# Windowed attention layers: per-head 64x32 array tiles, scores and attention output in shared PSUM banks, and a new order of the tensor engine's work

## The reference

```
# per layer: 16 heads of width 64, windows of 32 tokens
qkv = shift_tokens(x) @ Wqkv                 # 128 -> 3 x 1024
q, k = l2norm(q) * qs, l2norm(k) * ksc, then rotary
# each window of 32 queries sees 64 keys: its own window and the one before
sim  = einsum('bhwie,bhwje->bhwij', bq, bk2) * 8
attn = softmax(where(mask, -big, sim))
out  = einsum('bhwij,bhwje->bhwie', attn, bv2) @ Wo
x = out + x
x = (a * gelu(gate)) @ W2 + b2 + x           # a, gate = norm(shift_tokens(x)) @ W1 + b1
```

## Time and profile before

| | |
|---|---|
| timed runs, median | 4777.45 us |
| profiled execution, its own time | 4780.14 us |
| its span, first to last instruction | 4778.4 us |
| mean granted PE clock | 0.962 |
| layers phase, first to last mask product | 615.5 to 4096.0 us |
| one turn in the steady state | 35.67 us |

### The profile page before, as it was taken

One profiled execution on the slowest core, in us unless ns is written; L12 is line 12 of the kernel. 1 busy time (PEld: TensorE's weight loads), 2 busy tenths in 40 slices (PEclk: granted clock), 3 DMA queues, 4 the chain that ended last, 5 costly groups with the idle time before them and its releaser, 6 DMA issues. The chain is left out here.

```text
span 4778.4 us, 118285 instructions
## 1 busy us (share of the span) xinstructions
PE 4447.2 (93%) x45408; PEld 3473.8 (73%) x45408; DVE 3626.2 (76%) x6437; ACT 3028.2 (63%) x4718; POOL 1788.6 (37%) x966
## 2 busy tenths in 40 slices
PE   7999589999999999999999999999999999689999
PEld 2333268887788877888778887788778888468778
DVE  6887588888788887878878888788888888466554
ACT  5777357676767766676667676776767676333333
POOL 0000155554555544555455554455445555000000
PEclk9988799999999999999999999999999999889999
DMA  0000122222322222222222222222222222100000
GB/s 28 5 5 5 47 59 60 56 54 51 84 53 57 60 57 70 59 60 52 69 64 58 54 59 70 59 58 59 56 69 61 59 57 55 62 7 5 9 7 5
DMA packets 132797, 229.65 MB, mean 48 GB/s; under 512 B 29080, under 2 KB 33824, under 8 KB 131104
## 3 DMA queue, kind: packets, MB, share of 16 engines
q1 hardware_dynamic: 132256, 222.28, 17.8%
HBM read 29.23 MB, written 4.19 MB: 7 GB/s over the span
## 5 line engine op out<-in xcount | busy, mean ns | idle before, releaser
L660 POOL TENSOR_TENSOR qk_rotated<-qk_rotated,rotary_sines 128x1024 f32<-128x1024 f32 x384 | 923.5, 2405 | 1693.1 <-DVE rotary_sines L748 1693.1
L671 POOL TENSOR_TENSOR qk_rotated<-qk_rotated,rnorm 128x1024 f32<-128x1024 f32 x384 | 733.7, 1911 | 7.4
L756 DVE TENSOR_REDUCE qk_sumsq<-qk_squared 128x16 f32<-128x1024 f32 x384 | 467.4, 1217 | 296.5 <-ACT qk_squared L502 296.5
L221 PE MATMUL ps_proj<-qkv_w_hi,x_shifted_hi 128*128 128x512 f32 x1152 | 493.8, 429 | 38.7 <-DVE qkv_w_lo L716 24.0
L509 ACT ACTIVATE q_t<-ps_qk_t 128x512 f32<-128x512 f32 x384 | 229.7, 598 | 465.3 <-PE ps_qk_t L277 465.3
L738 DVE TENSOR_TENSOR qk_rotated<-ps_proj,rotary_scaled 128x1024 f32<-128x1024 f32 x384 | 467.4, 1217 | 7.6 <-ACT qk_squared L502 4.3
L748 DVE TENSOR_TENSOR rotary_sines<-ps_proj,rotary_scaled 128x1024 f32<-128x1024 f32 x384 | 466.0, 1213 | 1.7 <-POOL qk_rotated L660 1.7
L523 ACT ACTIVATE k_t_by_head<-ps_qk_t 64x512 f32<-64x512 f32 x768 | 452.1, 589 | 11.8 <-PE ps_qk_t L286 2.5
L223 PE MATMUL ps_proj<-qkv_w_hi,x_shifted_lo 128*128 128x512 f32 x1152 | 458.9, 398 | 0.0
L222 PE MATMUL ps_proj<-qkv_w_lo,x_shifted_hi 128*128 128x512 f32 x1152 | 457.4, 397 | 0.0
L502 ACT ACTIVATE qk_squared<-ps_proj 128x1024 f32<-128x1024 f32 x384 | 392.4, 1022 | 67.5 <-DVE qk_sumsq L756 49.8
(11 more groups left out here) (248 smaller groups left out, 9727.2 us busy)
## 6 DMA issues: line engine op xcount, KB each, us to landing
v_by_window<-v_tokens SPq DMA_DIRECT2D x1152, 128.0 KB, 2.4
v_by_window<-v_tokens SPq DMA_DIRECT2D x384, 64.0 KB, 2.1
v_by_window<-v_by_window SPq DMA_DIRECT2D x192, 64.0 KB, 2.0
qkv_w_raw<-in_layer_qk_dram SPq DMA_DIRECT2D x7, 1664.0 KB, 7.7
layer_w<-in_layer_w_dram SPq DMA_DIRECT2D x6, 580.5 KB, 3.8
layer_w<-in_layer_w_dram SPq DMA_DIRECT2D x6, 512.0 KB, 3.5
f_x<-in_x_dram SPq DMA_DIRECT2D x8, 256.0 KB, 6.2
x_attn<-f_y SPq DMA_DIRECT2D x8, 256.0 KB, 2.0
```

The costliest lines, as they stand in the source:

```text
L221: mm(out, hi, HI[:, o:o + 512], start=True, stop=False)
L660: tt(u, u, TB[:], ALU.add).then_inc(added, 1)
L671: tt(u, u, r.unsqueeze(3).broadcast_to((P, 2, 8, DH)), ALU.mult).then_inc(scaled, 1)
L756: nc.vector.reduce_sum(SS[:, 16 * i:16 * i + 16], SQ[:].rearrange("p (h e) -> p h e", e=DH), AX).then_inc(sumsq, 1)
```

## The change

Products: `score` and `pv` now treat each head by itself. The weights are 64 rows by 32 columns, the moving operand has 64 columns, and there are 32 products per group in place of 16 (64 records with their weight loads in place of 32). The two heads of a pair use the two halves of the rows. Scores and attention output of head z of each pair share one bank: `SA` is two banks, the first 256 columns of each are `S[z]`, the last 256 are `A[z]`. The mask product and `shift` become two products of 256 columns each. Keys and values lose the zero halves, and `k_t_out` is one copy of 128 partitions. All four transposes go through `TP`.

Order: `strips` waits for everything that scores and `pv` need ahead of the mask product. `out_t` moves ahead of `shift`; each of the projections `k0`, `v1`, `q1`, `k1` and `q0` is cut in two halves that stand around another piece, and `hidden01` is cut in `hidden0` and `hidden1` around `probs_t`. DVE does `norm_out` before `row_max`, and `row_max` also waits for `pv`. ACT does `out_t_out` before `exps`, and `high_part` moves up in slot 1.

```diff
-        TP, S, A, X = ps("ps_qk_t"), ps("ps_scores"), ps("ps_attention"), ps("ps_tail")
+        SA, TP, X = ps("ps_scores_attn", 2 * 512), ps("ps_transposed"), ps("ps_tail")
+        S = [SA[:, 512 * z:512 * z + 256] for z in range(2)]
+        A = [SA[:, 512 * z + 256:512 * z + 512] for z in range(2)]
...
+                for z in range(2):
+                    mm(S[z].rearrange("p (c k) -> p c k", k=DH), IDR[:], MASKR[:, g.t:g.t + 1, 0:DH].broadcast_to([P, 4, DH]), start=True, stop=False,
+                       skip_group_check=True)
                 for c in range(4):
-                    for w in range(4):
-                        q, k = g.t * P + WIN * w, base + WIN * w
-                        last = mm(S[WIN * w:WIN * w + WIN, c * P:(c + 1) * P], QT[:, 4 * g.half + c, q:q + WIN],
-                                  KD[:, :, 4 * g.half + c, k:k + 2 * WIN], start=False, stop=True, skip_group_check=True)
+                    for z in range(2):
+                        rows = slice(DH * z, DH * z + DH)
+                        for w in range(4):
+                            q, k = g.t * P + WIN * w, base + WIN * w
+                            last = mm(S[z][WIN * w:WIN * w + WIN, c * DH:(c + 1) * DH], QT[rows, 4 * g.half + c, q:q + WIN],
+                                      KT[rows, 4 * g.half + c, k:k + 2 * WIN], start=False, stop=True, skip_group_check=True)
...
+            def strips(scored, attended):
+                score_waits(scored)          # exps of the group before, q and k copied, halo
+                pv_waits(attended)           # probs copied, norm_out of the group before, values
+                score(scored)
+                pv(attended, scored.live)
...
+            def out_t(g, turned, scored):
+                if g.live:
+                    pe.wait_ge(o_norm, g.n + 1)
+                    if turned.live:
+                        pe.wait_ge(qt_out, turned.n + 1)
...
-                score(gs[0])
-                pv(ga[0])
-                q_t(gt[0])
-                shift(gs[0])
-                k0(n1)
-                out_t(ga[0])
-                k_t(gt[0])
-                v1(now, n1)
-                probs_t(gs[0])
+                strips(gs[0], ga[0])
+                q_t(gt[0], gs[0])
+                k0_first(n1)
+                out_t(ga[0], gt[0], gs[0])
+                shift(gs[0])
+                k0_second(n1)
+                k_t(gt[0], ga[0])            # now also waits for out_t_out
+                v1_first(now, n1)
+                probs_t(gs[0], gt[0], ga[0]) # now also waits for k_t_out
+                v1_second(now)
                 rstd_rows(h, e)
...
+                q_t(gt[1], gs[1])            # slot 1
+                q1_first(n1)
+                mean(e)
+                out_t(ga[1], gt[1], gs[1])
+                shift(gs[1])
+                q1_second(n1)
+                k_t(gt[1], ga[1])
+                hidden0(h, n1)
+                probs_t(gs[1], gt[1], ga[1])
+                hidden1(h)
...
+                hidden2(h, e)                # slot 2
+                out_t(ga[2], gt[2], gs[2])
+                shift(gs[2])
+                k1_first(n1, h)
+                k_t(gt[2], ga[2])
+                k1_second(n1)
...
+                wo_first(w)                  # slot 3
+                out_t(ga[3], gt[3], gs[3])
+                shift(gs[3])
+                q0_first(n2)
+                k_t(gt[3], ga[3])
+                q0_second(n2)
...
-                for h in range(2):           # ACT, k_t_out
-                    r = slice(DH * h, DH * h + DH)
-                    a(KD[r, h, 4 * g.half:4 * g.half + 4, base:base + P], TP[r, :].rearrange("p (c k) -> p c k", k=P),
-                      ACT.Copy).then_inc(kt_out, 1)
+                a(KT[:, 4 * g.half:4 * g.half + 4, base:base + P], TP[:].rearrange("p (c k) -> p c k", k=P), ACT.Copy).then_inc(kt_out, 1)
...
-                row_max(gs[0])               # DVE, slot 0; the other slots likewise
                 norm_out(ga[0])
+                row_max(gs[0], ga[0])
```

More of the change, by code:

```diff
@@ L214, in _, with project @@
             mm = nc.tensor.matmul
-            def project(m, t, x, bank, done):
-                for half in range(2):
+            def project(m, t, x, bank, done, halves=(0, 1)):
+                for half in halves:
                     out, o = bank[:, 512 * half:512 * half + 512], x * INNER + 512 * half
@@ L223, in project, with q0_first @@
                     last = mm(out, lo, HI[:, o:o + 512], start=False, stop=True)
-                last.then_inc(done, 1)
-            def q0(m):
+                    if half == 1:
+                        last.then_inc(done, 1)
+            def q0_first(m):
                 if m.live:
@@ L311, in shift @@
                     pe.wait_ge(nmax, g.n + 1)
[L312 to L315 removed]
+                    for z in range(2):
+                        last = mm(S[z].rearrange("p (c k) -> p c k", k=DH), IDR[:], NMX[:, 4 * z:4 * z + 4].unsqueeze(2).broadcast_to((P, 4, DH)),
+                                  start=False, stop=True, skip_group_check=True)
@@ L317, in probs_t @@
+                    last.then_inc(shifted, 1)
+            def probs_t(g, turned, attended):
                 if g.live:
                     pe.wait_ge(exped, g.n + 1)
+                    if turned.live:
+                        pe.wait_ge(kt_out, turned.n + 1)
+                    elif attended.live:
+                        pe.wait_ge(ot_out, attended.n + 1)
+                    after(pe, pt_out, g.n)
+                    for c in range(4):
+                        last = nc.tensor.transpose(TP[:, c * P:(c + 1) * P], E[:, g.k % 2, c * P:(c + 1) * P], IDENT[:])
+                    last.then_inc(pt_mm, 1)
@@ new lines, in pv @@
+            def pv(g, cleared):
+                if not g.live:
+                    return
+                for c in range(4):
+                    for z in range(2):
+                        rows = slice(DH * z, DH * z + DH)
+                        for w in range(4):
+                            o = c * P + WIN * w
+                            last = mm(A[z][WIN * w:WIN * w + WIN, c * DH:(c + 1) * DH], PT[rows, o:o + WIN],
+                                      V2[rows, 4 * g.t + w, 4 * g.half + c, :], start=(c == 0 and not cleared), stop=True,
+                                      skip_group_check=True)
+                last.then_inc(pv_mm, 1)
@@ L337, in out_t @@
[L337 to L342, removed]
+                        last = nc.tensor.transpose(TP[:, c * P:(c + 1) * P], O[:, c * P:(c + 1) * P], IDENT[:])
                     last.then_inc(ot_mm, 1)
@@ L389, in hidden, with hidden0 @@
                 last.then_inc(w1_mm, 1)
-            def hidden01(m, front):
+            def hidden0(m, front):
                 if m.live:
@@ L461, in turn @@
                 v0(n1)
-                score(gs[3])
-                pv(ga[3])
-                q_t(gt[3])
-                shift(gs[3])
+                strips(gs[3], ga[3])
+                q_t(gt[3], gs[3])
                 if j == B + 1 and more(layer):
@@ L604, in turn @@
                 q_t_out(gt[1])
+                high_part(n2)
+                out_t_out(ga[1])
                 exps(gs[1])
@@ L874, in turn @@
                 sum_squares(n1, 0)
+                norm_out(ga[1])
+                row_max(gs[1], ga[1])
+                normalize(h)
                 sum_squares(n1, 1)
-                row_max(gs[1])
-                norm_out(ga[1])
-                normalize(h)
                 cosines(n1, 1)
```

156 lines of the change are left out of this document (78 added, 78 removed).

## The result

The changed kernel took 5054.32 us in the median of four runs (5043.38 to 5058.78), the kernel before 4775.76 us beside it: a ratio of 1.0573, 95% interval 1.056 to 1.0585. The forecast was 4638 us, and the time lies far outside its range of 4500 to 4790.

What follows compares the result with a forecast made beforehand. PE was taken as the bound, with DVE 6 us behind in a turn. 1.56 us a turn over some 77 steady turns gave 120 us, layer changes 15, the rest about 5: 4640 profiled, 4638 forecast, range 4500 to 4790.

Steps and rivals of the forecast that it cites:

- Eight pairs of weight load and matmul at 7 ns give 0.055 too, so issue doesn't add: Score and pv strips: a 64-column round of eight tiles takes 0.055 us, saving 0.86 us a slot.
- 0.02 for the mask product: Mask product split in two: 0.02 us more a slot, and the same for shift, 0.04 together.
- the whole forecast gain of 1.56: Steady turn, slots 0 to 3: 0.27 + 0.14 + 0.63 + 0.52 = 1.56 us, 34.1 in place of 35.67.
- Against it: only a packet that lies wholly in the burst is used up so fast; most hold the 100 slower instructions of a slot too: PE's instruction fetch: argument against a wait for one 16 KB packet in each slot.
- the case: Rival, 5%: PE's instructions come too late in the strips, one packet wait a slot, 4.3 us a turn, 5030 us.
- The layout of the slots: All four slots: DVE's chains and waits for copies cut the products' net gain of 0.82 us a slot.
- the bank takes the gain: Rival, 8%: four transposes sharing TP, ACT 0.4 us late to one copy a slot, lose 1.6 us a turn: 4775.
- The two row halves run side by side: Strips: the halves overlap, gaining 0.86 us a slot; the rival that they don't had 7%, 4950 us.
- DVE's chain sets slots 0 and 1: Slots 0 and 1: v1_first at 5.27 and hidden0 at 6.73 wait for sines, leaving gains of 0.27 and 0.14 us.
- The copy of k is done once, and it hid on ACT: ACT: one copy of k for two saves 2.4 us a turn, counted at nothing because ACT has idle time.
- Records don't cost 28 ns each: Strips: rival, 3%, said records cost 28 ns each, 3.6 us a slot in place of 1.9, 5570 us in all.

Runs made afterwards that it cites:

- e1: The kernel before with each score and pv product cut in two of 64 columns on its old tiles, 256 strip instructions a slot: 4833.94 us, 1.0108.
- e6: The changed kernel with pv back on the old tiles and zero-padded values, 192 strip instructions a slot: 4985.59 us, 1.0431.
- e8: The changed kernel with 16 more pairs of variance products (128 PE instructions) once per loop body of 64 slots: 5151.91 us, 1.0773.
- e3: The changed kernel with PE and ACT in the old order, tiles, banks and norm_out ahead of row_max kept: 6026.15 us, 1.259.
- e2: The changed kernel with queries, keys, probabilities and values of the attention in bf16, half the strip instructions: 4615.21 us, 0.9652.
- e4: The changed kernel with old tiles, zero halves and two k copies, scores and attention a bank each; new order, waits and TP kept: 5075.32 us, 1.0617.
- e5: The old-tiles, new-order kernel (5075.32 us) with row_max ahead of norm_out again and without its wait for pv: 5027.42 us, 1.052.
- e9: The old-tiles, new-order, row_max-first kernel (5027.42 us) with probs_t and out_t transposed in the attention bank instead of TP: 4813.05 us, 1.0063.

## Why the prediction was wrong

**The step "Eight pairs of weight load and matmul at 7 ns give 0.055 too, so issue doesn't add".** It failed. A burst was read and taken for a rate. The first rounds of eight do keep the 7 ns. Then the records start at longer distances (8.3 ns and pauses), whose cause no run shows; in bf16, with half the records, 32 keep 7.2 ns. The two strips take 1.41 us in the median where 1.00 was laid out, and 0.02 for the mask product, which did not get longer: 0.39 us a slot, 1.56 a turn. That happens to equal the whole forecast gain of 1.56, and the undisturbed turn is indeed 35.68 us, as before. The slots say the same: 7.70, 9.37, 8.62 and 8.42 were forecast, 8.18, 9.66, 9.13 and 8.71 measured, 0.29 to 0.51 more each.

**The step "Against it: only a packet that lies wholly in the burst is used up so fast; most hold the 100 slower instructions of a slot too".** It failed, and this is the sign of the result. The prediction had the right quantities (62 bytes, 16 KB, a transfer of about 1 us, strips of about 1 us) and gave the case 5%. What counts is not which instructions a packet holds. It is how long the instructions that are left when its fetch starts keep PE busy, against the 2.15 to 3.02 us after which PE goes on. In dense products, whose matmuls start 0.23 us apart, that is far more than enough; in the two strips shown it was 0.7 and 0.8 us. A hole follows whenever the border falls so, in a third of the slots (21 of 64) and not in each: 204 us of the 278 that were lost. The rival's term was 4.3 us a turn, the measured one 204 / 96 = 2.1. It came to 5030 us, near the truth by luck, since it also kept the gain of 140 us that was not there. e1 (holes in the old kernel), e6 (192 instructions), e8 (borders moved), e3 (order changed, holes in the same slots) and e2 and e4 (none at half the number) show the cause between them.

**The waits of order and bank.** The layout of the slots was about right in sum: outside of mask and strips the medians grew by 1.97 us a turn (26.39 to 28.36), and the prediction had taken 1.72 off its 3.28. But it was read as a small discount on a gain. e4 shows what it is: on the old tiles order, waits and bank are a loss of 3.2 us a turn, which tiles and single copy of k just pay back. Of that 2.4 us are the one bank for four transposes (e5 to e9), 0.6 the maxima behind `pv` (e4 to e5), 0.2 the rest. The rival "the bank takes the gain" named the mechanism, and had 1.6 us for it. On the new tiles the bank was not measured apart.

**What held.** The two row halves run side by side (eight records under way 0.06 us after the first). DVE's chain sets slots 0 and 1: `v1_first` came 5.64 us after its mask product, 5.27 forecast, with a wait of 0.29 for the sines; the difference is the strips' 0.39. `hidden0` was laid out at 6.73 and came at 2135.79 - 2126.90 - 1.63 = 7.26, with a wait of 0.85 us for the sines. The copy of k is done once, and it hid on ACT. Records don't cost 28 ns each.

**The sum.** Before to after, 278 us: the undisturbed turn adds nothing (strips -1.92, the rest +1.97 and mask -0.07 us), the holes within `pv` 204 us. Some 70 us remain, spread over the means of all slots, slot 3 the most (rest 6.97 in the median, 7.34 in the mean). Two things in the trace make up nearly all of them. 17 more holes, 2.2 to 2.9 us after the start of a packet like the others, stand just behind the strips, ahead of the transposes of q:

```profile
PE ps_transposed L307 <- issue: 20.3, 17, 1.6
```

And the granted clock, of which the prediction had no term, fell more often. In the layers it was at half, the lower of its two levels (1.2 GHz), in 44 stretches, 167 us together; before in 18, 61 us, most of them at changes of layer. 38 of the 44 lie in a slot with a hole. A hole with such a stretch behind it, as a timeline and a window (the clock is the third number from the end):

```profile
1031.41 0.45 PE L384 MATMUL ps_scores_attn<-v_by_window,probs_t 64*32 64x64 f32 x30 [1.88 <-issue]
1032.68 1.91 PE L452 MATMUL ps_tail<-y_normed,layer_w 128*128 128x256 f32 x4
1031.85:1035.26 3.41, 3.41 (x15) 2.95 (x14) 3.29 (x6) 1.07 (x2) 0.00 (x0) 0.50 0.41 92
```

The same four products take 1.03 us at the full clock (2103.19). In slot 3, slots with a hole last 10.62 us in the median at the full clock and 12.53 with a stretch at half, where the holes are only 0.2 us longer. At half of the 106 us that came to it, the clock is worth up to 53 us (an estimate). That the holes bring the clock down is argued from where the stretches lie, not tested apart; e4, e5 and e9, which have no hole, have 7, 10 and 12 stretches.

## What to carry to other kernels

Count instructions, not only columns: in fp32 a product is two matmuls and two weight loads, and cutting it in smaller tiles can use up PE's instructions faster than they are fetched. Compare the work that PE has left when a packet's fetch starts with the 2.15 to 3.02 us that passed here until PE went on, look at the granted clock behind each hole, and look for "issue" as the cause of idle time within a group of products. A gain found in the first few records of a burst must be read over the whole burst, and when a bank is shared, price the hand-overs on the old tiles first.

## What the runs showed of the hardware

Matmul and weight-load pairs on eight 64x32 tiles started 7 ns apart at first and 8.3 ns later. The Trainium skill ("TensorE: Matmul & The Clock Gate", section "Wait — 56ns, not 53.3ns?") puts a floor of about 25 ns under the distance of two starts; between different tiles this trace does not agree with it, 32 bf16 products took 0.23 us, 7.2 ns each.

A packet of instructions (16 KB, some 256 of them) took 0.93 us to move ahead of the first hole shown, and in the 120 longer holes PE went on 2.15 to 3.02 us after its start. In the changed kernel this stopped PE within `pv` up to 2.2 us at a time, 122 times, and the place of the stops moved when 128 instructions were put in elsewhere.

In 38 of the slots with such a stop the granted clock stood at half for a stretch of 3.4 or 6.8 us. Four products in one of these stretches took 1.91 us in place of 1.03.
